# Last unit of a fused adaLN block: a split moved from GpSimd to VectorE, and the final projection, sums and stores taken tile by tile

## The reference, cut to what matters

```
x = x + ga * attn(layernorm(x) * (1 + ca) + sa)
h = layernorm(x) * (1 + cb) + sb
up_gate = einsum('bsd,hd->bsh', h, W1)          # 256 -> 1024
up_lin  = einsum('bsd,hd->bsh', h, W3)          # 256 -> 1024
hidden  = fwht(silu(up_gate) * up_lin)          # Walsh-Hadamard transform over the 1024
x = x + gb * einsum('bsh,dh->bsd', hidden, W2)  # 1024 -> 256
```

## Time and profile before

| what | value |
|---|---|
| timed, median of 3 runs | 277.26 us (276.52 to 277.75) |
| the profiled execution's own time | 275.44 us |
| its span, first to last instruction | 273.5 us |
| mean granted TensorE clock | 0.996 of full |
| PE busy | 252.9 us (92%) |
| DVE busy | 172.6 us (63%) |
| POOL busy | 136.6 us (50%) |
| ACT busy | 121.5 us (44%) |

### The profile page before, as it was taken

How to read it: one execution, slowest core, us unless ns; L and a number is a source line. 1 busy time by engine, 2 the same in 40 slices (tenths; PEclk the granted TensorE clock), 3 DMA queues, 4 the chain that set the end, 5 groups by cost and what they waited for, 6 DMA issues and landing times.

```text
span 273.5 us, 4983 instructions
## 1 busy us (share of the span) xinstructions
PE 252.9 (92%) x1888; PEld 238.5 (87%) x1888; DVE 172.6 (63%) x340; ACT 121.5 (44%) x249; POOL 136.6 (50%) x159
## 2 busy tenths in 40 slices
PE   1698897699999999999999999999999999999992
PEld 1566776599999898999999999999999999999992
DVE  3358897997766684667767756568648556562211
ACT  2427728564373335532642536534453356134320
POOL 3285182359334793254736373744347925434334
PEclk9999999999999999999999999999999999999998
DMA  6998401000100001000100010001100060000102
GB/s 208 351 384 316 153 4 38 1 2 0 42 0 2 0 2 40 0 2 1 41 0 2 0 38 2 0 4 37 41 2 0 2 192 2 0 0 2 41 0 77
DMA packets 11294, 13.89 MB, mean 51 GB/s; under 512 B 1156, under 2 KB 9348, under 8 KB 11016
## 3 DMA queue, kind: packets, MB, share of 16 engines
q1 hardware_dynamic: 11272, 13.58, 15.2%
HBM read 9.64 MB, written 2.11 MB: 43 GB/s over the span
## 4 chain that ended last, share of the span: by engine, by line
PE 78%; POOL 10%; DVE 4%; issue 3%; ACT 2%; DMA 2%; POOLq 0%; SPq 0%; ACTq 0%; DVEq 0%
PE pu L304 31%; PE pacc L304 13%; PE pd L304 7%; PE pa L304 6%; PE pb L304 4%; PE pc L311 3%; PE pc L304 3%; PE pstate L329 2%; POOL rso L793 2%; DMA wmod_sb<-wmod 2%; POOL yo L825 1%; POOL hid_lo L833 1%; PE pa L311 1%; PE pstate L304 1%; POOL rs L793 1%
## 5 line engine op out<-in xcount | busy, mean ns | idle before, releaser
L304 PE MATMUL pu<-h_hi,w_hi 128*128 128x256 f32 x256 | 73.1, 286 | 0.0
L304 PE MATMUL pu<-h_hi,w_lo 128*128 128x256 f32 x256 | 72.5, 283 | 0.0
L304 PE MATMUL pu<-h_lo,w_hi 128*128 128x256 f32 x256 | 72.5, 283 | 0.0
L833 POOL TENSOR_TENSOR hid_lo<-hid,hid_hi 128x512 fp32r<-128x512 f32 x32 | 41.3, 1296 | 49.8 <-ACT hid_hi L781 49.8
L304 PEld LDWEIGHTS pu<-h_hi,w_hi 128*128 128x128 f32 x256 | 49.1, 192 | 0.7 <-DVE h_lo L485 0.3
L304 PEld LDWEIGHTS pu<-h_lo,w_hi 128*128 128x128 f32 x256 | 49.1, 192 | 0.3
L304 PEld LDWEIGHTS pu<-h_hi,w_lo 128*128 128x128 f32 x256 | 49.1, 192 | 0.0
L304 PE MATMUL pacc<-w_hi,hid_hi 128*128 128x256 f32 x128 | 37.3, 291 | 0.7 <-POOL hid_lo L833 0.7
L304 PE MATMUL pacc<-w_lo,hid_hi 128*128 128x256 f32 x128 | 36.2, 283 | 0.0
L304 PE MATMUL pacc<-w_hi,hid_lo 128*128 128x256 f32 x128 | 36.2, 283 | 0.0
L776 ACT ACTIVATE silu<-pu 128x512 f32<-128x512 f32 x32 | 19.0, 594 | 31.5 <-PE pu L304 31.4
(11 more groups left out here) (136 smaller groups left out, 625.2 us busy)
## 6 DMA issues: line engine op xcount, KB each, us to landing
raw<-w SPq DMA_DIRECT2D x4, 512.0 KB, 9.9
out<-xres SPq DMA_DIRECT2D x8, 256.0 KB, 2.4
qb<-qkt SPq DMA_DIRECT2D x28, 64.0 KB, 2.0
xres<-x SPq DMA_DIRECT2D x1, 1536.0 KB, 13.4
raw_w<-w SPq DMA_DIRECT2D x1, 1024.0 KB, 7.9
wmod_sb<-wmod SPq DMA_DIRECT2D x1, 1024.0 KB, 9.8
gates<-gate_dram SPq DMA_DIRECT2D x1, 1024.0 KB
xres<-x SPq DMA_DIRECT2D x2, 256.0 KB, 4.3
```

The source lines that it names most:

```text
L304: mm = pe.matmul(ps, a, c, start=start and n == 0, stop=stop and n == len(ops) - 1, skip_group_check=True)
L833: pool.tensor_tensor(hid_lo[:, k % 2], hid32[:, k % 2], hid_hi[:, k % 2].bitcast(F32), ALU.subtract).then_inc(p_hid.sem, 1)
```

## The change

It concerns unit 7 alone. The low half of its last block, `7:hid.3`, is made by VectorE instead of GpSimd, with a semaphore of its own (`d_hend`). In this unit tile 1 accumulates in bank `pd` instead of the right half of `pacc` (`down_bank`). In `7:down.3` the loop order is turned around: all six matmuls of tile 0 first, then the six of tile 1, and tile 0's end is signalled by itself (`t_end`). VectorE multiplies each tile with the gate by itself; GpSimd adds tile 0 to the residual, VectorE adds tile 1; SyncE stores each tile with its own DMA.

```diff
+LAST = UNITS - 1
@@ ORDERS, ends of the DVE and POOL lists
-  DVE  "... 7:up.2 7:up.3 7:out"
+  DVE  "... 7:up.2 7:up.3 7:hid.3 7:out"
-  POOL "... 7:hid 7:hid.1 7:hid.2 7:hid.3 6:out 7:out"
+  POOL "... 7:hid 7:hid.1 7:hid.2 6:out 7:out"
...
+        def down_bank(u, j):
+            return pd[:, 0:D] if u == LAST and j else pacc[:, j * D:(j + 1) * D]
@@ SyncE
+                elif kind == "out" and u == LAST:
+                    for j, done in ((0, (p_out, LAST + 1)), (1, (d_xend, 1))):
+                        sp.wait_ge(done[0].sem, done[1])
+                        sp.dma_start(out[u // 2, par * UT + j * P:par * UT + (j + 1) * P], xres[:, u, j]
+                                     ).then_inc(stored.sem, 16)
...
-            sp.wait_ge(stored.sem, stored.after(UNITS - 1, 15))
+            sp.wait_ge(stored.sem, stored.after(UNITS, 15))
@@ TensorE, down
+                            if u == LAST:
+                                pe.wait_ge(d_br.sem, d_br.after(u))
...
-                    pe.wait_ge(p_hid.sem, p_hid.after(u, k))
-                    for n in range(2):
-                        for j in range(2):
+                    if (u, k) == (LAST, 3):
+                        pe.wait_ge(d_hend.sem, 1)
+                    else:
+                        pe.wait_ge(p_hid.sem, p_hid.after(u, k))
+                    if (u, k) == (LAST, 3):
+                        blocks_of = [(n, j) for j in range(2) for n in range(2)]
+                    else:
+                        blocks_of = [(n, j) for n in range(2) for j in range(2)]
+                    for n, j in blocks_of:
...
+                        if (u, k, n, j) == (LAST, 3, 1, 0):
+                            mm.then_inc(t_end.sem, 1)
@@ VectorE
+                elif kind == "hid" and (u, k) == (LAST, 3):
+                    dve.wait_ge(a_hid.sem, a_hid.after(u, k))
+                    split(d_hend, hid_lo[:, k % 2], hid32[:, k % 2], hid_hi[:, k % 2])
+                elif kind == "out" and u == LAST:
+                    dve.wait_ge(p_out.sem, p_out.after(u - 1))
+                    for j, done in ((0, (t_end, 1)), (1, (t_d, t_d.after(u, 3)))):
+                        dve.wait_ge(done[0].sem, done[1])
+                        dve.tensor_tensor(fin[:, j], down_bank(u, j), gates[:, b, 1], ALU.mult
+                                          ).then_inc(d_end.sem, 1)
+                    dve.wait_ge(d_end.sem, 2)
+                    dve.tensor_tensor(xres[:, u, 1], xres[:, u, 1], fin[:, 1], ALU.add).then_inc(d_xend.sem, 1)
@@ GpSimd
-                elif kind == "hid":
+                elif kind == "hid" and (u, k) != (LAST, 3):
...
+                elif kind == "out" and u == LAST:
+                    pool.wait_ge(d_end.sem, 1)
+                    pool.tensor_tensor(xres[:, u, 0], xres[:, u, 0], fin[:, 0], ALU.add).then_inc(p_out.sem, 1)
```

More of the change, by code:

```diff
@@ L224, in adaln_block_kernel @@
         d_fin, p_out = sem("d_fin"), sem("p_out")
+        t_end, d_end, d_xend, d_hend = (sem(n) for n in "t_end d_end d_xend d_hend".split())
         def tile_of(u, k):
@@ L465, in step @@
                             pe.wait_ge(d_fin.sem, d_fin.after(u - 1))
+                            if u == LAST:
+                                pe.wait_ge(d_br.sem, d_br.after(u))
                         else:
                             pe.wait_ge(d_w2.sem, 4)
-                    pe.wait_ge(p_hid.sem, p_hid.after(u, k))
-                    for n in range(2):
-                        for j in range(2):
[L471 to L475, removed]
+                    if (u, k) == (LAST, 3):
[7 more added lines that the diff above has]
+                    for n, j in blocks_of:
+                        of = slice(n * UT + j * P, n * UT + (j + 1) * P)
+                        mm = three(down_bank(u, j),
+                                   [((hid_hi[:, k % 2, of], hid_lo[:, k % 2, of]),
+                                     (w2_hi[:, 2 * k + n], w2_lo[:, 2 * k + n]))],
+                                   start=(k == 0 and n == 0 and (j == 0 or u == LAST)), stop=(k == 3 and n == 1))
+                        if (u, k, n, j) == (LAST, 3, 1, 0):
+                            mm.then_inc(t_end.sem, 1)
                     mm.then_inc(t_d.sem, 1)
```

## The result

The changed kernel takes 274.27 us, the median of 17 runs (272.57 to 277.58); the kernel before takes 276.52 us in its 17 runs (275.48 to 277.75). The ratio is 0.9913, 95% interval 0.9892 to 0.9934: 1.8 to 3.0 us less, clearly more than the 0.5% that can be told from no change. The profiled execution took 273.0 us, its span is 271.15 us (273.51 before).

The account below looks back on a forecast made before the run. The prediction saw the end bound by a chain through five engines; 0.61 + 1.16 - 0.15 + 0.3 = 1.9 us off 277.26 gave 275.4 us, own range 274.7 to 276.1, eight-in-ten range 274.5 to 276.7.

Parts of the forecast that it names:

- signs of being wrong: Second landing 2.4 us or more, VectorE's low half stretched past 266.6, or TensorE's pace dropping in unit 7's `down`.
- Step 1: Unit 7's last low half on VectorE ends sooner than on GpSimd, so `down.3` starts 0.61 us earlier.
- Step 2: Products and sums by tile around `down.3`: last sum done at 269.17 instead of 270.94, 1.16 us beyond Step 1.
- Step 3: SyncE's issue of tile 1's store stands behind tile 0's issue: 0.15 us back.
- Step 4: Landing of the last store: half the bytes to move, 0.3 us saved.
- the second store did not land late: Rival at the last store: issued with the first on its way, lands late, 0.6 to 1.2 us back; 12%.
- the sum of unit 6 did not run long: Rival on GpSimd: unit 6's sum takes up to 1.82 us, leaving 0.1 us of Step 1, 275.9; 7%.
- the stores overlapped: Against the rival that the last two stores go in series, 2.1 us each, giving 277.2; 5%.
- the change of bank cost nothing: Against the rival that TensorE stalls at twelve `pacc`/`pd` changes in unit 7's `down`, up to 0.28 us each, 278.5; 4%.
- step 1's cover: GpSimd's sum of unit 6, moved ahead, overlaps VectorE's low half but stretches it only to 266.47, before 266.52: nothing lost.

Follow-up runs that it names:

- low half alone: The kernel before with only unit 7's last low half moved from GpSimd to VectorE; ratio to before 0.9966, tail 9.45 us.
- the change again: The changed kernel run once more, unedited; ratio to the kernel before 0.9921, tail 8.06 us.
- late sum: The change, with GpSimd's sum of unit 6 waiting until `down.1` of unit 7 has ended; ratio to before 0.9963, tail 8.61 us.
- buffer alone: The change, with the last block's halves in buffers of their own, GpSimd's order kept; ratio to before 0.994, tail 8.05 us.
- tiles alone: The change without moving the low half, which GpSimd makes as before; ratio to before 0.9956, tails 9.21 and, run again, 8.86 us.

## Why the prediction was wrong

The step that failed is the base: "its difference is then taken off the median, 277.26, which is 1.8 us above that execution". None of the three runs behind that median was a low one: with 14 more runs of the same kernel the median is 276.52, which is the lowest of the three, and beside the experiments it was 276.78 (17 runs) and 276.46 (29 runs). So the base was 0.74 us too high. That is most of the 1.13 us between 275.4 and 274.27; the other 0.39 us are gain beyond the forecast, since the medians differ by 2.25 us. Off 276.52 the forecast's 1.9 us give 274.6, just inside the range. The sign stood in the numbers at hand: the profiled execution, a fourth one, took 275.44, below all three. It is in fact below all 17, and the change's profiled execution is the second lowest of its 17, so the two that were compared both lie at the quick end. The range allowed for too little of this, "a median fall lower by half of that", and only for the median to come, where the one to start from is as uncertain. By its own terms (277.26 - 2.1 - 0.6) the forecast's own range should also have begun at 274.6 and not at 274.7.

The mechanism was right, and none of the signs of being wrong that the prediction names came. Its sum, term by term, from `down.1`'s first matmul on:

- *Step 1*, 0.61 us: the first weights of `down.3` came 3.73 us after it before and 3.11 us after it now, 0.62 us. The low half alone kept all of it to the end.
- *Step 2*, 1.16 us: the last sum was done at 7.49 us (270.94) before and 5.73 us (268.81) now, 1.76 in all, 1.14 without step 1. No run separates its parts (the loop order, the bank, the products, the shared sums).
- *Step 3*, 0.15 us back: the last issue came 0.12 us behind the sum instead of 0.03, so 0.09 us.
- *Step 4*, 0.3 us: 1.99 - 0.62 - 1.14 + 0.09 = 0.32 us, and one store for both takes back steps 3 and 4 together (0.28 us).

Together 1.99 us in the tail against 1.9 foreseen. The times say 1.8 to 3.0 us, and 1.6 to 2.7 us for the change again (0.9902 to 0.9941 of 276.78); the tail lies inside both. That their middles, 2.4 and 2.2 us, are above 1.99, as is the 2.25 us between the medians, is not explained and may be chance.

Of the rivals, the second store did not land late (1.8 us), the sum of unit 6 did not run long (1.30 us), the stores overlapped, and the change of bank cost nothing (0.12 us). The rule on which step 1's cover rested, that a VectorE instruction on two SBUF operands waits out a running GpSimd one, held in three kernels: 1.22 us with the late sum, 1.41 with the buffer alone, 0.54 with the tiles alone. VectorE ended 0.55 or 0.56 us behind GpSimd at 128x512 and 0.28 us at 128x256, each 0.13 or 0.14 us less than the instruction takes alone. The Trainium skill's page SBUF — State Buffer, section "SBUF: two separate sides", says that whichever of the two starts first holds the other off for its whole instruction, and these runs agree with it, but for that 0.14 us. Its section "The DMA setup-cost knee" asks for the largest single transfer where transfers are the limit; for the last store here the runs say otherwise, since two halves end 0.28 us sooner than one whole. An estimate from its 2 us and 436 GB/s would be 2.6 us for 256 KB and 2.3 us for 128 KB; the runs show 2.1 and 1.8, so only the difference of 0.3 us agrees.

## What to carry to other kernels

At the end of this program the 0.61 us taken from one instruction that nothing overlapped came through in full. So look there: cut the last pieces by tile, let another engine take the parallel one, and split the last store. Look at what else moves in the DMA queues at that time; in the tiles alone the stores lost up to 0.4 us there. When work goes from GpSimd to VectorE, look at what GpSimd then runs beside it: a sum moved by half a microsecond gave back 0.54 of 0.62 us, and an earlier start bought with a buffer was worth nothing until that sum was out of the way. Take the base of a forecast from all executions known, the profiled one too, and widen the range by how far their median can be off.

## What the runs showed of the hardware that was not expected

A store's landing can hang on one late stream of packets: with 8 KB of instructions loading in the same stretch, unit 6's store took 2.8 us in both runs of the tiles alone, where it took 2.1 or 2.2 us in the change. The length alone would prove little, since the eight stores of the kernel before take up to 3.0 us; it is the 16th closing packet, 0.55 us or more behind the other 15, that shows it, and the load as its cause stays argued. The end of the program can repeat better than the whole: from one execution to the next the change stood 1.17 us apart at `down.1` and took 8.07 and 8.06 us from there. The same two executions of the tiles alone differ by 0.35 us in the tail, and all of that lies behind the last issue.
